# A vision tower of two layers: a norm of a norm with one root, tiles normed one by one, resident expert vectors and a new order at the second attention's end

## What is computed

```python
h = SCALE * einsum(patches, weight)                       # 512 x 256
h = h + attn0(_ln(h))           # 16 heads of 64, causal, scores clamped by 50*tanh(s/50), softmax
h = h + moe0(_ln(h))            # 8 experts, top 2, silu(x w1) * (x w3), then w2; width 1024
h = h + attn1(_ln(h))           # linear attention, random features cos/sin of 16 heads
x = _ln(h)                      # the outer norm of the second experts
logits = x @ Wg                 # top 2, softmax, times alpha
for e in range(8):
    hdn = _layernorm(x, ln_w[e], ln_b[e])                 # the inner norm: a norm of x
    out += (gelu(hdn @ fc1_w[e] + fc1_b[e]) @ fc2_w[e] + fc2_b[e]) * comb[:, e]
h = h + out
```

## Time and profile before

| what | us |
|---|---|
| median of three runs | 410.11 |
| lowest and highest | 408.48, 411.88 |
| the profiled execution | 412.24 |
| its span in the trace | 410.6 |
| PE busy | 369.8 (90%) |
| DVE busy | 234.1 (57%) |
| POOL busy | 199.7 (49%) |
| ACT busy | 165.0 (40%) |

### The profile page before, as it was taken

One profiled execution on the slowest core, in us unless ns is written; L12 is line 12 of the kernel. 1 busy time (PEld: TensorE's weight loads), 2 busy tenths in 40 slices (PEclk: granted clock), 3 DMA queues, 4 the chain that ended last, 5 costly groups with the idle time before them and its releaser, 6 DMA issues.

```text
span 410.6 us, 9235 instructions
## 1 busy us (share of the span) xinstructions
PE 369.8 (90%) x3456; PEld 320.7 (78%) x3456; DVE 234.1 (57%) x797; ACT 165.0 (40%) x402; POOL 199.7 (49%) x132
## 2 busy tenths in 40 slices
PE   4999999999869999999997979999967799788886
PEld 3888888888769999999975867888946698777772
DVE  1852254543264554455568246679878556677675
ACT  1145354443124444433341468776600434333330
POOL 0013912004077788998960760033436336777743
PEclk9999999999889999999998998999965689999995
DMA  8999700000015788788138200000000457677423
GB/s 293 402 417 437 311 2 15 13 2 26 2 38 182 275 303 300 314 338 333 40 104 328 85 0 2 0 2 2 26 2 13 140 177 267 241 273 255 138 77 111
DMA packets 15731, 64.53 MB, mean 157 GB/s; under 512 B 2769, under 2 KB 7889, under 8 KB 10961
## 3 DMA queue, kind: packets, MB, share of 16 engines
q1 hardware_dynamic: 14160, 59.88, 38.9%
q0 software_dynamic: 1536, 4.20, 3.2%
HBM read 54.70 MB, written 9.37 MB: 156 GB/s over the span
## 4 chain that ended last, share of the span: by engine, by line
PE 62%; DMA 12%; DVE 11%; ACT 4%; POOL 4%; issue 4%; SPq 2%; DVEq 0%; POOLq 0%
DMA wslot<-blob_dram 10%; PE ps L520 8%; PE ps L861 7%; PE ps L863 6%; PE ps L862 6%; PE ps L527 4%; PE ps L578 4%; PE ps L555 3%; PE ps L1533 3%; PE ps L1321 3%; PE ps L1333 3%; PE ps L1309 3%; PE ps L1167 2%; PE ps L539 2%; POOL area_q L1063 2%
## 5 line engine op out<-in xcount | busy, mean ns | idle before, releaser
L861 PE MATMUL ps<-xeT,wslot 128*128 128x160 bf16 x384 | 83.4, 238 | 8.7 <-DVE xeT L931 6.7
L862 PE MATMUL ps<-xeT,wslot 128*128 128x160 bf16 x384 | 83.0, 237 | 0.0
L1063 POOL TENSOR_TENSOR area_q<-wslot 128x4096 bf16<-128x4096 f32 x8 | 56.1, 7014 | 24.8 <-DMA wslot<-blob_dram 24.8
L1069 POOL TENSOR_TENSOR area_w<-wslot 128x2048 bf16<-128x2048 f32 x16 | 57.6, 3601 | 17.6 <-DMA wslot<-blob_dram 17.5
L861 PE MATMUL ps<-hid,wslot 128*128 128x160 bf16 x256 | 54.6, 236 | 0.0
L862 PE MATMUL ps<-hid,wslot 128*128 128x160 bf16 x256 | 54.5, 236 | 0.0
L863 PE MATMUL ps<-hid,area_w 128*128 128x160 bf16 x256 | 54.4, 235 | 0.0
L863 PE MATMUL ps<-xeT,area_q 128*128 128x160 bf16 x256 | 54.0, 234 | 0.0
L861 PEld LDWEIGHTS ps<-xeT,wslot 128*128 128x128 bf16 x384 | 38.3, 100 | 13.9 <-issue 5.9
L949 DVE TENSOR_TENSOR ps<-act_g,ps 128x160 f32<-128x160 f32 x64 | 21.0, 329 | 38.5 <-ACT act_g L907 38.5
L943 DVE TENSOR_TENSOR hid<-ps,hid 128x160 bf16<-128x160 f32 x128 | 39.7, 315 | 1.1
(11 more groups left out here) (207 smaller groups left out, 826.4 us busy)
## 6 DMA issues: line engine op xcount, KB each, us to landing
wslot<-blob_dram SPq DMA_DIRECT2D x8, 2048.0 KB, 8.1
wslot<-blob_dram SPq DMA_DIRECT2D x16, 1024.0 KB, 6.2
wslot<-blob_dram SPq DMA_DIRECT2D x8, 1031.0 KB, 5.1
slots_dram<-hid SPq DMA_DIRECT2D x8, 544.0 KB, 12.5
xe<-slots_dram SPq DMA_DIRECT2D x14, 128.0 KB, 2.5
slots_dram<-ye SPq DMA_DIRECT2D x14, 128.0 KB, 1.8
area_x<-x_dram SPq DMA_DIRECT2D x4, 384.0 KB, 6.1
area_w<-wq_dram SPq DMA_DIRECT2D x1, 1024.0 KB, 8.9
```

Source lines behind the costliest of these rows:

```text
L861: nc.tensor.matmul(out, w_high[:, s, high_at:high_at + P], x_high, start=first, stop=False)
L862: nc.tensor.matmul(out, w_high[:, s, high_at:high_at + P], x_low, start=False, stop=False)
L1063: nc.gpsimd.tensor_tensor(w_low1[L][:, s, :], wslot[:, s, 0:SECOND[L]], w_high[:, s, 0:SECOND[L]], ALU.subtract).then_inc(main[L].low1_rea ...
L1069: nc.gpsimd.tensor_tensor(w_low2[:, s, :], wslot[:, s, o:o + KF * D], w_high[:, s, o:o + KF * D], ALU.subtract).then_inc(main[L].low2_read ...
```

## The change

1. `refine` has five narrow instructions instead of seven: the variance is scaled beforehand (`ONCE`), and the constants are folded.
2. The outer and the inner norm of the second experts become one root. With v the variance of h, the norm of the norm divides by the root of (1 + eps) v + eps squared (`TWICE`). The inner statistics, their refining and the tile `xn` between them are gone; the result goes from h to `xin`.
3. The root of the outer norm alone, needed for `gap`, is taken for four tiles at once by `outer_roots` (nine instructions), on DVE in the second experts, after the hidden step of expert 0.
4. `norm2_dve` norms tile by tile; `LAST_BANK` of tile 1 moves from 4 to 5.
5. In the first attention, POOL refines the last tile but DVE applies it, and the slots of tile 2 are taken later.
6. The end of `order1()` is reordered: the last "kernel" ahead of the addition, "first" and "back" early and between the other steps, each tile's slots right behind its places. POOL scatters a tile before it norms the next.
7. The vectors of all experts are loaded once at the start into `vec`; second halves of weights are 1024 KB instead of 1031, and DVE waits for none of them.
8. SP requests rows right behind the first half of the weights and the second half as soon as PE ends the expert (`y_full`), ahead of the store.
9. DVE's experts are written out instead of looped, and the copy of expert 5's results stands inside the hidden step of expert 6.

```diff
-V_LNW, V_LNB, V_B1, V_B2 = W1, W1 + KD, W1 + 2 * KD, W1 + 2 * KD + KF
+V_LNW, V_LNB, V_B1, V_B2 = 0, KD, 2 * KD, 2 * KD + KF
+VEC = 3 * KD + KF
+ROOT_SCALE = (256.0 / 3.0)**2
+ONCE = (LN_EPS, ROOT_SCALE)
+TWICE = ((1.0 + LN_EPS) * ROOT_SCALE, LN_EPS**2 * ROOT_SCALE)
...
+            if twice:
+                st.step(nc.vector.tensor_scalar(var[:, t:t + 1], mv[:, t, 1:2], *TWICE, ALU.mult, ALU.add))
+            else:
+                st.step(nc.vector.tensor_scalar(var[:, t:t + 1], mv[:, t, 1:2], *ONCE, ALU.add, ALU.mult))
...
-            step(eng.tensor_scalar(q, w, -0.5, 1.5, ALU.mult, ALU.add))
-            step(eng.tensor_scalar(y, y, q, None, ALU.mult))
+            step(eng.tensor_scalar(y, w, -3.0, y, ALU.add, ALU.mult))
             step(eng.tensor_scalar(w, y, v, y, ALU.mult, ALU.mult))
-            step(eng.tensor_scalar(q, w, 0.375, -1.25, ALU.mult, ALU.add))
-            step(eng.tensor_scalar(q, q, w, 1.875, ALU.mult, ALU.add))
-            done(eng.tensor_scalar(y, y, q, None, ALU.mult))
+            step(eng.tensor_scalar(w, w, -40.0 / 3.0, w, ALU.add, ALU.mult))
+            done(eng.tensor_scalar(y, w, 80.0, y, ALU.add, ALU.mult))
...
+        def outer_roots(st):
+            v, y, w = outer_var[:], outer_rstd[:], outer_work[:]
+            st.step(nc.vector.tensor_scalar(v, mv[:, :, 1], *ONCE, ALU.add, ALU.mult))
...
+                elif step == "apply":
+                    dve.wait_ge(rstd_ready, 1)
+                    norm_apply(nc.vector, t, h, xn, ln_done[1])
...
-        LAST_BANK = (3, 4, 1, 2)
+        LAST_BANK = (3, 5, 1, 2)
...
+                if f == BEHIND and between is not None:
+                    between()
...
-            rows_of_next(0, 0, 16, first_rows)
+            def rows_of(n, rows=next_rows):
+                split_rows_in_dve(dve, m, n, n % 2, vec[:, n, :], rows)
...
+            rows_of(0, first_rows)
             split_hidden_dve(dve, m, 0)
-            rows_of_next(1, 1, 16)
-            with dve.Fori(0, E // 2 - 1) as it:
...
+            if L == 1:
+                outer_roots(st)
+                gaps_dve(st, outer_rstd)
+            rows_of(1)
+            for n in range(1, E - 2):
+                split_hidden_dve(dve, m, n)
+                rows_of(n + 1)
+                rows_out(n - 1)
+            split_hidden_dve(dve, m, E - 2, lambda: rows_out(E - 3))
+            rows_of(E - 1)
+            rows_out(E - 2)
             split_hidden_dve(dve, m, E - 1)
...
                     load_first(L, blob, e + 2, e % 2)
+                    load_rows(sp, m, e + 2, e % 2)
+                    sp.wait_ge(m.y_full, KD * (e + 1))
+                    load_second(L, blob, e + 2, e % 2)
                 if e:
                     store_rows(e - 1, (e - 1) % 2)
-                if e + 2 < E:
-                    sp.wait_ge(m.yT_ready, KD * (e + 1))
-                    load_rows(sp, m, e + 2, e % 2)
-                    load_second(L, blob, e + 2, e % 2)
...
+            for t in range(NT):
+                gathered_dve(dve, st, 0, t)
+                last_back_dve(dve, st, 0, t)
+                norm_tile(dve, st, t, h, xn, ln_done[2])
```

More of the change, by code:

```diff
@@ L487, in order0 @@
             yield "logit", NT - 1, 0
-            yield "slot", NT - 2, 0
             yield "back", 1, 0
@@ L491, in order0 @@
             yield "back", NT - 2, 0
+            yield "apply", NT - 1, 0
             yield "place", NT - 1, 0
+            yield "slot", NT - 2, 0
             yield "slot", NT - 1, 0
@@ L1039, in moe_dve @@
             more = overflow(dve, L)
[L1040 removed]
+            rows_out(E - 1)
             with dve.If(more):
@@ L1253, in order1 @@
                     yield "kernel", n - 1
-                for step, behind in (("onT", 7), ("out", 8), ("norm", 8), ("rT", 9), ("logit", 10), ("place", 11),
-                                     ("slot", 11), ("inner", 11)):
+                for step, behind in (("onT", 7), ("out", 8), ("add", 8), ("norm", 8), ("rT", 9), ("logit", 10),
+                                     ("place", 11), ("slot", 11)):
                     if n >= behind and (n - behind) % 4 == 0 and (step, n) != ("onT", 4 * NT - 1):
@@ L1260, in order1 @@
             yield "out", last - 1
-            yield "norm", last - 1
             yield "sums", end - 2
             yield "kernel", end
+            yield "add", last - 1
+            yield "norm", last - 1
             yield "sums", end - 1
@@ L1266, in order1 @@
             yield "rT", last - 1
+            yield "first", 0
             yield "divide", last
+            yield "logit", last - 1
             yield "onT", last
[L1269 to L1271 removed]
+            yield "back", 0
+            yield "first", 1
+            yield "place", last - 1
+            yield "slot", last - 1
             yield "out", last
+            yield "back", 1
+            yield "add", last
             yield "norm", last
[L1274 removed]
             yield "rT", last
[L1276 to L1278 removed]
+            yield "first", 2
             yield "logit", last
[L1280 to L1283 removed]
             yield "back", 2
             yield "xin", last
+            yield "place", last
             yield "first", last
             yield "back", last
[L1288 removed]
             yield "slot", last
@@ L1410, in attn1_dve @@
                                             ALU.mult).then_inc(on1_ready, 1)
-                elif step == "out":
+                elif step == "add":
                     dve.wait_ge(wo_full[1], n + 1)
@@ L1482, in _ @@
                 scatter(pool, 0, t, xn)
-            for t in range(NT - 2, NT):
-                pool.wait_ge(outer_guess, t - (NT - 2) + 1)
-                refine(nc.gpsimd, newton[:, 1, :], own.step, t, own.step)
-                norm_apply(nc.gpsimd, t, h, xn, ln_done[1])
+            pool.wait_ge(outer_guess, 1)
+            refine(nc.gpsimd, newton[:, 1, :], own.step, NT - 2, own.step)
+            norm_apply(nc.gpsimd, NT - 2, h, xn, ln_done[1])
+            pool.wait_ge(outer_guess, 2)
+            refine(nc.gpsimd, newton[:, 1, :], own.step, NT - 1, lambda ins: ins.then_inc(rstd_ready, 1))
             for t in range(NT - 2, NT):
```

167 lines of the change are left out of this document (56 added, 111 removed).

## The result

The changed kernel takes 395.43 us, the median of 5 runs (394.84 to 400.33), beside 410.11 for the kernel before: ratio 0.963, 95% interval 0.958 to 0.967. The profiled execution took 397.13 us, its span is 395.4. A second measurement on another chip, where the kernel before takes 412.94 us, gave 0.9635 (0.9594 to 0.9675).

The account below looks back on a forecast made before the run. It took PE as full in the first experts, DVE's chain as the bound at the second attention's end, and a loop without PE in the second experts. Terms summed to -16.4 us, 410.11 to 393.7 us; range 389 to 401.5.

Parts of the forecast that it names:

- Between the layers, -3.5: Between the layers: norming each tile alone starts PE's transposes sooner and holds the clock, saving 3.5 us.
- -1.9: Between the layers: the saving in us that remains if the clock falls all the same.
- Rival 3: Between the layers: the last tile's norm decides, +6.3 us on that term, 400.0 us in all; chance 0.04.
- End of the second attention, -5.4: End of the second attention: 10.0 us leave DVE's chain, 4.6 us of new waits come, saving 5.4 us.
- Expert 0, -3.4: Expert 0, second experts: earlier scatters remove PE's 1.7 us wait, and the clock's second fall goes, saving 3.4 us.
- Roots, +1.0: After hidden 0, second experts: eleven narrow DVE instructions take 2.2 us, PE covers about 1.2, costing 1.0 us.
- Experts 2 to 7, -4.4 and -1.2: Second experts: DVE no longer waits for the weights' transfer, saving 4.4 us, and 1.2 before the last expert.
- the copy of expert 5, +0.5: Hidden step of expert 6, second experts: the moved copy stands ahead of steps PE waits for, costing 0.5 us.
- At nothing: Parts put at 0 us, such as fewer refining steps, one more small load, the bank move and earlier weight requests.
- 1: Second experts: the transfer bounds anyway through POOL's low part, so 4.4 and 1.2 us stay: 399.3 us; chance 0.10.
- 2, the clock: Clock falls sooner in the attention's end, in the projection and twice in expert 0: 399.4 us; chance 0.14.
- 4: Both expert stages: fetching DVE's written-out instructions costs some 2 us per expert, 24 us: 418 us; chance 0.03.

Follow-up runs that it names:

- changed again: The changed kernel itself, with no edit, measured a second time on another chip: ratio 0.9635 to the kernel before.
- late, spread, fill: Changed kernel with GpSimd's third and fourth halves after DVE's values, outer roots spread over expert 0's hidden steps, four unread matmuls before the first experts' last products: 391.35 us.
- old order: The changed kernel with the one root kept but the steps at the end of the second attention in their old order: 401.24 us, ratio 0.9723.
- SP's old order: The changed kernel with the vectors resident but SP's requests in the order of the kernel before: 395.59 us, ratio 0.9588.

## Why the prediction was right, and where it was not

The total, 393.7 us against 395.43, is well inside the range, but two misses of opposite sign hide in it. By its terms, against the profiles:

- **Between the layers, -3.5: measured +0.4, and +1.8 behind it.** Two steps failed. The first is "With so short a pause after L767 the clock should hold": it had fallen already, at 215.3 us, within the products, and PE's transposes started at 221.37 and not near 218.3. What made it fall is not shown; the pause of 0.83 us ahead of the products was there in the kernel before too, and there it held over them. Where it held, the stretch took 24.64 us ("changed again") and 24.85 ("late, spread, fill"), 3.4 and 3.2 less than before, so durations and order were right. The fall alone does not make the miss: the text's own "-1.9" for it was missed too. The second step is that the forecast stopped at PE's door. It priced DVE's later last tile at 0.6 us and asked only who waits for the tile on PE; GpSimd's four halves wait for it too. They ended 3.0 us later, and DVE's values met them. Rival 3 ("last tile's norm decides") was given 0.04 and dismissed because PE queues the tiles; it was right about the tile and wrong about the engine. In "changed again", where the clock held, PE then waited 5.65 us, 4.7 longer than in the first profile: more than the term.
- **End of the second attention, -5.4: measured -8.2.** The mechanism was right: the old order gives 17.4 us, so the norm is worth 4.8 and the order 3.4. The term was mis-sized by the clock, 0.97 over the stretch where the kernel before had 0.61: DVE's new waits, put at 4.6 us with PE at the lower clock, came to 1.4 (0.36, 0.33, 0.55 and 0.18). The text had this case at -7.8.
- **Expert 0, -3.4: measured -3.5.** The wait for the rows and the second fall of the clock went (one fall is left, 310.9 to 317.7 us), and "old order", with the same four scatters but 1.1 us nearer to the scaling of expert 0, brought a wait of 1.8 us back. So the gain hangs on when they start, as the term said.
- **Roots, +1.0: measured +1.2**, by taking them off the path.
- **Experts 2 to 7, -4.4 and -1.2, and the copy of expert 5, +0.5: measured -6.0 in all** (56.98 to 50.96), the copy +0.66 of it. The loop was read rightly from the earlier trace rows, and the resident vectors alone do open it, as the text said ("SP's old order"). What it didn't see is that SP's new order alone does as much. Nor was the copy's move needed: the 1.7 us of the earlier trace rows went with the loop, and the "-1.2" and the "+0.5" were one question.
- **At nothing.** The first products of the first experts started 0.2 us sooner (120.33 against 120.55) and their last result came 0.4 us later, within what kernels differ by that are the same there. The tail's -1.3 was not forecast; it is within that too.
- **Rivals.** 1 is out: no period above 8.39 names GpSimd. 2, the clock, came true in the projection, not in the attention's end. 4 is out: 8.39 us with the experts written out.

Against the forecast of -16.4 the first term lost 5.7 us and the start 0.4; the other terms won 3.6 and the tail 1.3: -15.2. That the total came within 2 us of the forecast is luck in so far as the 5.7 and the 3.6 have unrelated causes.

## What to carry to other kernels

When an edit makes one result earlier and another later, list every engine that waits for the later one, not only the one whose wait you remove: here the first normed tile came 2.7 us sooner and the last 2.6 later, and GpSimd, which PE's waits do not name, took the gain back through DVE. A DVE instruction with its operands in SBUF should not be placed where GpSimd runs an instruction as long as these halves; if it must, delay GpSimd by a wait. And when two edits both break a loop, undo each alone before crediting one.

## What the runs showed of the hardware

A DVE instruction that starts while GpSimd makes one of these halves, a TENSOR_TENSOR that reads 2048 columns in SBUF for 3.60 us, stands still until the half ends, however small it is itself: 4 columns took 1.90 and 3.45 us beside halves of 3.60 us, 128 columns 1.55 and 1.84, 256 columns 3.72, and each ended within 0.3 us of GpSimd's end. The profile books this as busy time of DVE, not as a wait; only a duration far from that of the same line elsewhere gives it away. This held for instructions with both inputs in SBUF and for a TENSOR_SCALAR with one; those with an input in PSUM (L968, L1392) ran beside the same halves at their usual 0.33 us, and 1.28 us for two. The Trainium skill, page "SBUF — State Buffer", section "Who interferes with whom", says so: whoever issues first gets the shared pair of ports for the whole instruction, and the other fully blocks; this concerns instructions with two SBUF inputs beside a GpSimd instruction that reads SBUF, as the halves do, and the two-port modes that a TENSOR_SCALAR can take. The traces agree in each case above. They don't agree everywhere: beside GpSimd's norms of one tile, which read SBUF too, an instruction with both inputs in SBUF kept its usual time, as in "late, spread, fill":

```profile
299.10 1.22 POOL L264 TENSOR_SCALAR area_y<-h,mv,rstd 128x256 f32<-128x256 f32 x1
```

```profile
299.72 0.18 DVE L389 TENSOR_TENSOR oh<-const,i2f 128x16 f32<-128x16 f32 x1
```

So what is shown is shown for the TENSOR_TENSOR halves, not for every GpSimd instruction.

The clock's fall is not a property of the program alone: the same kernel ran the same eight products at 2.4 GHz in one profile (0.69 us a pair) and mostly at 1.2 in the other (1.22), with the same wait of 0.83 us ahead of them. What decides between the two is not shown.
